# A two-layer image kernel: planes stored once, loads of 16 rows, and the calls of slots 0 to 6 in another order on three engines

## The chip, the core and the metric

The kernel runs on one core of a Trainium2 chip. Its time is the device time of one launch in microseconds (us): the median of three runs. The core has TensorE (PE), VectorE (DVE), ScalarE (ACT), GpSimd (POOL) and SyncE (SP), whose queue issues nearly all DMAs here. Each engine works through its own list of instructions in order, and semaphores order them against each other.

## What is computed

Eight images of 128 channels and 64x64 pixels go through two layers. The first splits an image into four bands of 32x32 (Haar), runs a sparse attention with 8 heads on the low band, a depthwise and a 1x1 convolution with group norms on the other three, puts the bands together and adds a feed-forward part. The second is a full attention over all 4096 pixels with queries and keys of 16 numbers.

```
# layer 0, the attention on the low band: N = 1024, 8 heads, hd = 16
q = _l2norm(q); k = _l2norm(k)
attn = einsum('bhnd,bhmd->bhnm', q, k) * hd ** -0.5
_, idx = top_k(attn, N // 2)          # keep 512 of 1024 per row
attn = where(mask(idx), attn, -1e9)
out = einsum('bhnm,bhmd->bhnd', softmax(attn), v)
...
# layer 1: n = 4096, R = 16
q = einsum('rc,bcn->bnr', Wq, xf) + bq
k = einsum('rc,bcn->brn', Wk, xf) + bk[:, None]
v = einsum('oc,bcn->bon', Wv, xf) + bv[:, None]
attn = softmax(einsum('bnr,brm->bnm', q, k) / 4.0)
out = einsum('bcm,bnm->bcn', v, attn)
out = gamma[0] * (einsum('oc,bcn->bon', Wo, out) + bo[:, None]) + xf
```

## The kernel before

**Stages.** The work of layer 0 for image b runs together with that of layer 1 for image b−1. The program is: `between(0,0)` (opens image 0), `slots(0)` (layer 0 alone), a loop over six images of `between(b-1,b)` and `slots(b)`, the same two once more for the last image, then `between` (closes layer 0 of the last image) and `slots(8)` (layer 1 alone). `between` does all that is not attention: the convolutions, the norms, the feed-forward part, and the projections of queries, keys and values of both layers. `slots` has eight slots and what follows them. Slot h takes head h of layer 0 and chunk h of layer 1: 512 of the 4096 queries.

**Precision.** Queries and keys are split into three bf16 planes whose sum is the fp32 value. A score is the sum of six products of planes, named by `TERMS` as pairs (plane of q, plane of k), so a matmul contracts over 6x16 = 96 rows, written to DRAM from the planes and read back in the order of `TERMS` (QK0 for layer 0, `work` in the trace's names; QP1 and KP1, `QP` and `KP`, for layer 1). Three more rows hold the threshold of a query in layer 0 (from TPT) and its maximum in layer 1 (from MPT), so that the exponential's argument comes out of the matmul itself: 99 rows.

**A head of layer 0**, the calls and the line each has in the trace. PE `score(h,i)` (L446), i = 0 to 7, makes 128x1024 scores; ACT `evict(h,i)` (L1175) copies them out with their sum. DVE `centre(h,k)` (L1671, T<-SUM) makes a first threshold of half k, that is of tiles 4k to 4k+3, from those sums; ACT `count(h,round,i)` (L1183) counts the scores above it in three rounds, and DVE `update` (L1701) moves it. DVE `apart` (L1743), `excess` (L1726, L1729), `flip` (L1751) and `eight` (L1760) find the eight scores nearest to it; `match`, `middle` and `threshold` (to L1843) the exact one. PE `turn` (L490), ACT `turned` (L1217) and three DMAs (L368) bring it as TPT's rows into QK0. Then PE `half_t` (L514) makes the scores again, now turned, ACT `half_e` (L1235) takes the exponential, DVE `half_m` (L1857) sets it to zero below the threshold, and PE `weigh` (L524) multiplies by the values.

**A chunk of layer 1.** PE `maxima(h,k)` (L548), k = 0 to 31, makes 128x512 scores and DVE `maxima` (L1928) reduces them to a maximum. Both go through one PSUM bank, so PE's next one waits for DVE's reduction. DVE `parts`, PE `maxrow` (L555), ACT `maxrow` (L1251, writes MPT) and three DMAs (L324) bring the maxima into QP1. Then PE `l1_score(h,j)` (L566), j = 0 to 15, ACT `l1_exp` (L1243) and PE `l1_weigh(h,j)` in two halves of eight matmuls (L582); in the end DVE `l1_norm` (L1950), PE `l1_turn` (L594) and DVE `l1_out` (L1960), and SP stores the output (L337).

**What sets the order.** Nobody schedules: each engine's list is written out by hand as calls. For slots 0 to 6 of images 1 to 7 that is `search` and the loop body that follows it on PE, a loop body on ACT, and `search` on DVE; they hold calls of four neighbouring heads and chunks. `first`, `closing`, `alone` and `chunks` are other lists, for the rest. `score` waits for a free pair of two PSUM banks that it shares with `half_t`, and `l1_score` has two other pairs. SP's list in a slot is: TPT's rows, loads of layer 1's input, MPT's rows for the next chunk, `load_head(h+3)` (L279), the store of finished output. In `between` SP stores layer 0's planes (`store_planes`, L286), loads heads 0 to 2, stores layer 1's planes (L406), loads QP1 and KP1 (L410), and stores X1 (L413).

## Time and profile before

| | |
|---|---|
| median of three runs | 5667.28 us |
| lowest and highest | 5665.16 and 5668.21 us |
| span of the profiled execution | 5667.7 us |
| one image (`between` and eight slots) | 668 us |
| one of the 49 slots, `l1_out` to `l1_out` | 63.7 to 63.8 us, up to 64.7 |
| granted TensorE clock, mean; in the slot read | 0.91; 1.00 |
| DMA over the span | 35 GB/s of mean traffic, 200 MB |

The profile is one execution; its span is the time from the first to the last instruction and stands 0.4 us over the median of the runs. Busy times are sums per engine; DMA-issuing and waiting instructions do not count as busy. A slot is read best along DVE, from one `l1_out` to the next.

### The profile page before, as it was taken

What the parts mean: (1) busy time and instruction counts of PE and PEld (TensorE: products, weight loads), DVE (VectorE), ACT (ScalarE), POOL (GpSimd) and SP (SyncE); (2) the same over time, 40 slices, a digit from 0 to 9 for tenths busy, and PEclk for the clock granted to TensorE, in tenths of its full rate; (3) what the DMA queues carried; (4) which work ended last, traced back from release to release, by engine and by line L of the source; (5) the groups of instructions that cost most, each with busy time, mean ns of one, the idle gap of its engine ahead of it and who ended that gap; (6) DMA issues with size and microseconds to landing.
All of it is one profiled execution on the core that took longest, in us unless ns stands there. A gap on an engine that the chain in (4) does not pass through costs nothing.

```text
span 5667.7 us, 92692 instructions
## 1 busy us (share of the span) xinstructions
PE 4766.2 (84%) x30180; PEld 3123.3 (55%) x30180; DVE 4618.9 (81%) x9087; ACT 4256.4 (75%) x6779; POOL 250.6 (4%) x125
## 2 busy tenths in 40 slices
PE   4444899988999889988999889998899889997799
PEld 2001366654666456663666546664466636664588
DVE  4887799987999789986999879997799879996553
ACT  3883699948998499966999489884899669994333
POOL 2001000010000200010000100002000100000000
PEclk7555799998999989998999989999899989998899
DMA  1001200012001110012000120011100120001100
GB/s 68 7 11 50 74 15 16 15 56 76 16 20 43 59 43 18 16 61 74 15 15 13 58 76 16 20 43 50 51 16 18 59 75 15 15 13 43 36 12 16
DMA packets 104805, 199.97 MB, mean 35 GB/s; under 512 B 36632, under 2 KB 41656, under 8 KB 100184
## 3 DMA queue, kind: packets, MB, share of 16 engines
q1 hardware_dynamic: 104280, 193.56, 11.1%
q8 instruction: 257, 4.21, 0.3%
q14 instruction: 268, 2.20, 0.1%
HBM read 110.61 MB, written 82.05 MB: 34 GB/s over the span
## 4 chain that ended last, share of the span: by engine, by line
PE 41%; DVE 23%; ACT 15%; issue 14%; SPq 3%; DMA 3%; DVEq 0%; ACTq 0%; POOL 0%; POOLq 0%
PE PS L582 16%; ACT work L1183 7%; PE PS L548 5%; DVE M L1760 4%; DVE MX L1928 4%; PE PS L566 4%; ACT work L1243 3%; DVE work L1751 3%; PE PS L514 3%; PE PS L524 3%; DVE work L1743 2%; PE PS L1057 2%; ACT arena L1175 2%; DVE arena L1857 2%; DMA work<-TPT 1%
## 5 line engine op out<-in xcount | busy, mean ns | idle before, releaser
L582 PEld LDWEIGHTS PS<-V,work 128*128 128x128 f32 x16384 | 2106.7, 193 | 155.8 <-issue 7.0
L582 PE MATMUL PS<-V,work 128*128 128x129 f32 x16384 | 2125.2, 277 | 2.5 <-ACT work L1243 1.2
L1183 ACT ACTIVATE work<-arena,T 128x1024 bf16<-128x1024 f32 x1504 | 1725.8, 1150 | 22.7 <-DVE T L1671 18.8
L1928 DVE TENSOR_REDUCE MX<-PS 128x1 f32<-128x512 f32 x2048 | 1399.3, 687 | 249.6 <-PE PS L548 233.9
L1243 ACT ACTIVATE work<-PS 128x1024 f32<-128x1024 f32 x1024 | 1046.8, 1024 | 334.0 <-PE PS L566 332.3
L548 PE MATMUL PS<-KP,QP 96*128 96x512 bf16 x2048 | 845.5, 414 | 137.3 <-DVE MX L1928 95.3
L566 PE MATMUL PS<-QP,KP 99*128 99x512 bf16 x2048 | 624.6, 387 | 77.5 <-ACT work L1243 54.2
L1175 ACT ACTIVATE arena<-PS 128x1024 f32<-128x1024 f32 x512 | 523.2, 1022 | 216.7 <-PE PS L446 209.5
L1857 DVE SCALAR_TENSOR_TENSOR arena<-PS,work 128x512 f32<-128x512 f32 x896 | 606.2, 684 | 67.3 <-ACT work L1235 65.3
L1760 DVE MAX8 M<-work 128x8 f32<-128x512 f32 x1024 | 648.4, 682 | 1.0
L1235 ACT ACTIVATE work<-PS 128x512 f32<-128x512 f32 x896 | 530.8, 601 | 119.9 <-PE PS L514 116.1
L548 PEld LDWEIGHTS PS<-KP,QP 96*128 96x128 bf16 x2048 | 200.5, 98 | 543.8 <-DVE MX L1928 419.1
L446 PE MATMUL PS<-work 96*128 96x512 bf16 x1024 | 350.5, 428 | 175.2 <-ACT arena L1175 167.2
L514 PE MATMUL PS<-work 99*128 99x512 bf16 x896 | 337.3, 388 | 93.7 <-DVE arena L1857 54.2
L1743 DVE TENSOR_SCALAR work<-arena,T 128x1024 f32<-128x1024 f32 x512 | 378.4, 745 | 2.3
L1751 DVE TENSOR_SCALAR work<-work,FL 128x1024 uint32<-128x1024 uint32 x512 | 375.9, 747 | 1.0
L524 PE MATMUL PS<-arena,VT 128*17 128x256 f32 x4096 | 321.4, 411 | 10.0 <-DVE arena L1849 5.8
L566 PEld LDWEIGHTS PS<-QP,KP 99*128 99x128 bf16 x2048 | 185.0, 99 | 222.6 <-ACT work L1243 126.5
L1183 ACT ACTIVATION_READ_ACCUMULATOR work<-arena,T 128x1 f32 x1504 | 302.9, 201 | 0.0
L446 PEld LDWEIGHTS PS<-work 96*128 96x128 bf16 x1024 | 80.4, 102 | 329.9 <-ACT arena L1175 272.2
L514 PEld LDWEIGHTS PS<-work 99*128 99x128 bf16 x896 | 83.2, 98 | 222.1 <-DVE arena L1857 127.0
L2614 POOL TENSOR_TENSOR work<-work 128x1024 f32<-128x1024 f32 x8 | 22.5, 2814 | 3509.9 <-DMA work<-in_x 3509.9
(193 smaller groups left out, 4160.8 us busy)
## 6 DMA issues: line engine op xcount, KB each, us to landing
scr<-work SPq DMA_DIRECT2D x96, 256.0 KB
work<-scr SPq DMA_DIRECT2D x128, 192.0 KB, 2.8
work<-in_x SPq DMA_DIRECT2D x16, 1024.0 KB, 7.7
arena<-in_x SPq DMA_DIRECT2D x8, 2048.0 KB, 9.9
scrX<-arena SPq DMA_DIRECT2D x8, 2048.0 KB, 14.2
XR<-scrX SPq DMA_DIRECT2D x64, 256.0 KB, 2.8
out<-YO SPq DMA_DIRECT2D x64, 256.0 KB, 2.0
scrL<-work SPq DMA_DIRECT2D x24, 512.0 KB, 2.6
```

Source lines behind the costliest of these rows:

```text
L514: mm(PS[:, c, :], kp(h)[0:KA, 128 * mt:128 * mt + 128], qp(h)[0:KA, 512 * c:512 * c + 512], start=True, stop=True).then_inc(s["st" if c el ...
L548: mm(PS[:, maxbank(c, k, l0), :], QP1[0:KS, c * 512 + 128 * i:c * 512 + 128 * i + 128], KP1[0:KS, 512 * w:512 * w + 512], start=True, stop ...
L566: last = mm(PS[:, pairbanks(k, l0) + t, :], KP1[0:KA, 128 * mt:128 * mt + 128], QP1[0:KA, j * 512:j * 512 + 512], start=True, stop=True)
L582: last = mm(PS[:, 5 + i // 2, 136 * (i % 2):136 * (i % 2) + 129], P1[:, (16 * j + k) % 3, t, 128 * i:128 * i + 128], V1[:, mt, :], start=( ...
L1175: A(scores(h, i), bank2(0), ACT.Copy, scale=0.25, accum_out=SUM[:, h % 2, i:i + 1]).then_inc(s["eva"], 1)
L1183: A(junk[:, m % 2, :], scores(h, i), ACT.Sign, scale=-1.0, bias=T[:, h % 2, i:i + 1], accum_out=CA[:, h % 2, i:i + 1]).then_inc(s["ca"], 1)
L1235: A(JA[:, mt % 2, 512 * c:512 * c + 512], PS[:, c, :], ACT.Exp, scale=0.25).then_inc(s["e" if c else "eh"], 1)
L1243: A(P1[:, (16 * j + k) % 3, :, :].rearrange("p t n -> p (t n)"), PS[:, u:u + 2, :].rearrange("p a n -> p (a n)"), ACT.Exp, scale=0.25).the ...
L1751: cp.did(V.tensor_scalar(JDu[:, c, :], JDu[:, c, :], FL[:, h % 2, i:i + 1].bitcast(u32), None, ALU.bitwise_xor))
L1760: cp.did(V.max(M8[:, i, a, :], JD[:, c, 512 * a:512 * a + 512]))
L1857: V.scalar_tensor_tensor(scores(h, mt)[:, 512 * c:512 * c + 512], PS[:, c, :], 0.0, JA[:, mt % 2, 512 * c:512 * c + 512], ALU.is_ge, ALU.m ...
L1928: V.reduce_max(MX[:, c % 2, i, w:w + 1], PS[:, maxbank(c, k, l0), :], AX.X).then_inc(s["mr"], 1)
```

## The change

**A, layer 0's planes.** `TERMS` has another order. `scr0` holds each plane once, so three stores of 128 rows x 4 KB take the place of twelve, and each head is loaded by 12 DMAs of 16 rows x 2 KB, one for each plane of each term, instead of two of 96 rows. PE's waits for a head count 192 instead of 32. For head 0 the loads of planes 0 and 1 (ten) start when these two have landed, and plane 2's two parts are copied from the planes in SBUF. Heads 1 and 2 are loaded behind layer 1's loads.

**B, layer 1's planes.** `scr1` is [3, 32, 4096]; each plane is stored by four DMAs when it is made, and QP1 and KP1 are loaded by 12 DMAs of 16 rows x 8 KB: the ten parts of planes 0 and 1 when those have landed, then the two of plane 2. Before, 12 DMAs of 16 rows x 4 pieces of 2 KB were issued when all three planes had landed.

**C, the call lists** of the 49 slots on PE, ACT and DVE hold the same calls in another order (116, 66 and 88 calls). The other lists are unchanged.

```diff
-TERMS = [(0, 0), (0, 1), (1, 0), (1, 1), (0, 2), (2, 0)]
+TERMS = [(0, 0), (0, 1), (0, 2), (1, 0), (1, 1), (2, 0)]
-        scr0 = nc.dram_tensor("scr0", [2, NH, len(TERMS), HD, N0], bf16, kind="Internal").ap()
-        scr1 = nc.dram_tensor("scr1", [3, 128, N0], bf16, kind="Internal").ap()
+        scr0 = nc.dram_tensor("scr0", [3, 128, 2, N0], bf16, kind="Internal").ap()
+        scr1 = nc.dram_tensor("scr1", [3, 32, N1], bf16, kind="Internal").ap()
-            def load_head(h):
+            def load_head(h, parts=(0, 1, 2)):
                 done = s["hq%d" % (h % 3)]
-                for w in range(2):
-                    sp.dma_start(QK0[0:KS, h % 3, w, :], scr0[w, h].rearrange("j d n -> (j d) n")).then_inc(done, 16)
+                d = slice(HD * h, HD * h + HD)
+                for j, pair in enumerate(TERMS):
+                    for w, t in enumerate(pair):
+                        if t in parts:
+                            sp.dma_start(QK0[HD * j:HD * j + HD, h % 3, w, :], scr0[t, d, w, :]).then_inc(done, 16)
+            def load_planes(parts):
+                for w, dst in ((1, KP1), (0, QP1)):
+                    for j, pair in enumerate(TERMS):
+                        if pair[w] in parts:
+                            sp.dma_start(dst[HD * j:HD * j + HD], scr1[pair[w], HD * w:HD * w + HD, :]).then_inc(s["qp1"], 16)
+            def store_plane(n, t, made):
                 sp.wait_ge(s[made], (n + 1) * 2)
+                sp.dma_start(scr0[t].rearrange("p w n -> p (w n)"), PT[:, t, :]).then_inc(s["scrw"], 16)
+            def head0_late():
                 for j, pair in enumerate(TERMS):
+                    for w, t in enumerate(pair):
+                        if t == 2:
+                            sp.dma_start(QK0[HD * j:HD * j + HD, 0, w, :], PT[0:HD, 2, w * N0:w * N0 + N0]).then_inc(s["hq0"], 16)
...
                 if opn:
-                    store_planes(n, 0, "p0")
-                    store_planes(n, 1, "p1")
-                    store_planes(n, 2, "p2")
+                    store_plane(n, 0, "p0")
+                    store_plane(n, 1, "p1")
                     sp.wait_ge(s["vt"], (n + 1) * 2)
                     sp.sem_inc(s["free"], 1)
-                    sp.wait_ge(s["scrw"], (n + 1) * 192)
-                    for h in range(3):
+                    sp.wait_ge(s["scrw"], n * 48 + 32)
+                    load_head(0, (0, 1))
+                    store_plane(n, 2, "p2")
+                    head0_late()
+                if fin:
+                    for a, made in enumerate(("p10", "p11", "p12")):
+                        sp.wait_ge(s[made], f + 1)
+                        for j in range(4):
+                            sp.dma_start(scr1[a][:, N0 * j:N0 * j + N0], PT1[32 * j:32 * j + 32, a, :])                                .then_inc(s["scrw1" if a < 2 else "scry1"], 16)
+                    sp.wait_ge(s["scrw1"], (f + 1) * 128)
+                    load_planes((0, 1))
+                    sp.wait_ge(s["scry1"], (f + 1) * 64)
+                    load_planes((2,))
+                if opn:
+                    sp.wait_ge(s["scrw"], (n + 1) * 48)
+                    for h in range(1, 3):
                         load_head(h)
...
@@ PE, tail of a slot
+                    l1_weigh(h - 1, 15, (0,))
+                    last_weigh(h, 7)
+                    l1_weigh(h - 1, 15, (1,))
                     maxrow(h)
-                    last_weigh(h, 7)
-                    l1_weigh(h - 1, 15, (0,))
-                    l1_weigh(h - 1, 15, (1,))
...
                     score(h + 1, 0)
...
                     l1_turn(h - 1)
+                    score(h + 1, 1)
...
```

How the three lists change where one slot ends and the next begins. ACT, from the next to last `half_e` of a head to the first exponential of the next chunk (L1235 `half_e`, L1183 `count`, L1251 `maxrow`, L1175 `evict`, L1243 `l1_exp`), before:

```order
L1235 ACTIVATE work<-PS 128x512
L1182 REGISTER_ALU
L1183 ACTIVATE work,CA<-arena,T 128x1024
L1235 ACTIVATE work<-PS 128x512
L1250 REGISTER_ALU
L1251 ACTIVATE MPT<-PS 12x128
L1203 ISA
L1175 ACTIVATE arena,SUM<-PS 128x1024
L1240 REGISTER_ALU
L1243 ACTIVATE work<-PS 128x1024
```

After, from the last `half_e` (L1247 there; L1194 `count`, L1263 `maxrow`, L1186 `evict`, L1255 `l1_exp`):

```order
L1247 ACTIVATE work<-PS 128x512
L1193 REGISTER_ALU
L1194 ACTIVATE work,CA<-arena,T 128x1024
L1193 REGISTER_ALU
L1194 ACTIVATE work,CA<-arena,T 128x1024
L1193 REGISTER_ALU
L1194 ACTIVATE work,CA<-arena,T 128x1024
L1262 REGISTER_ALU
L1263 ACTIVATE MPT<-PS 12x128
...
L1186 ACTIVATE arena,SUM<-PS 128x1024
L1252 REGISTER_ALU
L1255 ACTIVATE work<-PS 128x1024
```

Three counts now stand between the last `half_e` and MPT's copy. The rows left out are the first of two evictions and what waits ahead of each, so two evictions now stand ahead of the exponential. DVE, from the last part of `l1_norm` (L1950) over `l1_out` (L1960) to `centre` of the next head (L1671), before:

```order
L1950 TENSOR_TENSOR ON<-PS,RD 128x256 x2
L1685 REGISTER_ALU
L1726 TENSOR_SCALAR EC<-CA 128x4
L1729 TENSOR_SCALAR FL<-EC 128x4
L1760 MAX M<-work 128x8 x2
L1960 SCALAR_TENSOR_TENSOR YO<-PS,gbo,XR 128x512
L1743 TENSOR_SCALAR work<-arena,T 128x1024
L1928 TENSOR_REDUCE MX<-PS 128x1
L1751 TENSOR_SCALAR work<-work,FL 128x1024 x2
...
L1928 TENSOR_REDUCE MX<-PS 128x1
L1692 ISA
L1671 TENSOR_SCALAR T<-SUM 128x4
```

After (each line number is 12 higher):

```order
L1962 TENSOR_TENSOR ON<-PS,RD 128x256 x2
L1755 TENSOR_SCALAR work<-arena,T 128x1024
L1697 REGISTER_ALU
L1738 TENSOR_SCALAR EC<-CA 128x4
L1741 TENSOR_SCALAR FL<-EC 128x4
L1755 TENSOR_SCALAR work<-arena,T 128x1024
L1972 SCALAR_TENSOR_TENSOR YO<-PS,gbo,XR 128x512
L1763 TENSOR_SCALAR work<-work,FL 128x1024
L1940 TENSOR_REDUCE MX<-PS 128x1
...
L1940 TENSOR_REDUCE MX<-PS 128x1
L1704 ISA
L1683 TENSOR_SCALAR T<-SUM 128x4
```

Both `apart` calls are ahead of `l1_out`, and `centre` stands behind the second reduction, where it stood behind the fourth. PE, from the last `half_t` of a head (L514) to the second score of the next (L446), before:

```order
L514 MATMUL PS<-work 128x512
L555 MATMUL PS<-identb,MP 12x128
L573 REGISTER_ALU
L582 MATMUL PS<-V,work 128x129 x8
L524 MATMUL PS<-arena,VT 17x256 x12
L473 REGISTER_ALU
L446 MATMUL PS<-work 128x512 x2
L594 MATMUL PS<-cons,ON 128x128 x4
L562 REGISTER_ALU
L566 MATMUL PS<-QP,KP 128x512 x2
...
L463 REGISTER_ALU
L446 MATMUL PS<-work 128x512 x2
```

After (each line number is 17 higher):

```order
L599 MATMUL PS<-V,work 128x129 x8
L572 MATMUL PS<-identb,MP 12x128
L490 REGISTER_ALU
L463 MATMUL PS<-work 128x512 x2
L541 MATMUL PS<-arena,VT 17x256 x12
L611 MATMUL PS<-cons,ON 128x128 x4
L480 REGISTER_ALU
L463 MATMUL PS<-work 128x512 x2
L541 MATMUL PS<-arena,VT 17x256 x4
...
L579 REGISTER_ALU
L583 MATMUL PS<-QP,KP 128x512 x2
```

The halves of `l1_weigh` (L599) are ahead of `maxrow` (L572), the first score (L463) is right behind it, and `l1_score` (L583) comes last.

## Rows read from the trace of the kernel before

**Rows 1.** the page: the span; busy time by engine.

```profile
span 5667.7 us, 92692 instructions
...
PE 4766.2 (84%) x30180; PEld 3123.3 (55%) x30180; DVE 4618.9 (81%) x9087; ACT 4256.4 (75%) x6779; POOL 250.6 (4%) x125
```

**Rows 2.** stretches: length; busy PE, PEld, DVE, ACT, POOL; granted clock, DMA share, GB/s.

```profile
961.68:991.96 30.28, 26.75 (x185) 18.74 (x184) 28.79 (x62) 28.69 (x48) 0.00 (x0) 1.00 0.06 19
991.96:997.56 5.60, 4.77 (x35) 3.74 (x33) 3.78 (x10) 5.35 (x10) 0.00 (x0) 1.00 0.01 2
997.56:1025.51 27.95, 27.25 (x215) 19.32 (x213) 26.52 (x55) 25.21 (x44) 0.00 (x0) 1.00 0.07 19
961.68:1025.51 63.83, 58.77 (x430) 41.79 (x428) 59.09 (x123) 59.25 (x100) 0.00 (x0) 1.00 0.06 17
```

**Rows 3.** DVE's waits, 997.56 to 1025.51: for whom, us, times, longest.

```profile
DVE MX L1928 <- PE PS L548: 1.1, 2, 0.8
DVE YO L1960 <- PE PS L594: 0.3, 1, 0.3
DVE arena L1857 <- ACT work L1235: 0.3, 1, 0.3
```

**Rows 4.** timeline of DVE, same slot: start, us, line, operation.

```profile
961.68 0.75 DVE L1960 SCALAR_TENSOR_TENSOR YO<-PS,gbo,XR 128x512 f32<-128x512 f32 x1
962.35 0.74 DVE L1743 TENSOR_SCALAR work<-arena,T 128x1024 f32<-128x1024 f32 x1
...
970.43 0.16 DVE L1671 TENSOR_SCALAR T<-SUM 128x4 f32<-128x4 f32 x1
```

**Rows 5.** timeline of ACT, same slot; in brackets idle before, releaser.

```profile
957.37 0.61 ACT L1235 ACTIVATE work<-PS 128x512 f32<-128x512 f32 x1
957.84 0.25 ACT L1251 ACTIVATE MPT<-PS 12x128 bf16<-12x128 f32 x1
960.79 1.02 ACT L1175 ACTIVATE arena<-PS 128x1024 f32<-128x1024 f32 x1 [2.70 <-PE PS L446]
...
968.38 0.20 ACT L1175 ACTIVATION_READ_ACCUMULATOR arena<-PS 128x1 f32 x1
...
992.86 1.13 ACT L1183 ACTIVATE work<-arena,T 128x1024 bf16<-128x1024 f32 x1
...
996.59 0.60 ACT L1235 ACTIVATE work<-PS 128x512 f32<-128x512 f32 x1 [0.25 <-PE PS L514]
```

**Rows 6.** timeline of SP's DMA issues, same slot: MPT's rows, load_head.

```profile
958.12 1.97 SPq L324 DMA_DIRECT2D QP<-MPT  x3
960.21 0.83 SPq L279 DMA_DIRECT2D work<-scr  x2
```

**Rows 7.** timelines, image 1's first slot: MPT's copy, l1_score waiting for its rows.

```profile
699.41 0.27 ACT L1251 ACTIVATE MPT<-PS 12x128 bf16<-12x128 f32 x1 [0.98 <-PE PS L555]
...
702.87 1.03 PE L566 MATMUL PS<-QP,KP 99*128 99x512 bf16 x2 [2.61 <-DMA QP<-MPT]
```

**Rows 8.** timeline of PE, same slot: l1_score, and a half of l1_weigh.

```profile
961.48 0.60 PE L566 MATMUL PS<-QP,KP 99*128 99x512 bf16 x2
...
1019.04 1.06 PE L582 MATMUL PS<-V,work 128*128 128x129 f32 x8
```

**Rows 9.** timelines, last boundary: first and last load (SP), PE's wait.

```profile
5273.74 0.33 SPq L410 DMA_DIRECT2D QP<-scr  x1
...
5278.80 0.43 SPq L410 DMA_DIRECT2D KP<-scr  x1
...
5288.58 1.01 PE L548 MATMUL PS<-KP,QP 96*128 96x512 bf16 x2 [13.08 <-DMA KP<-scr]
```

**Rows 10.** timelines at the boundaries of images 0, 2 and 3.

```profile
108.86 1.00 ACT L1175 ACTIVATE arena<-PS 128x1024 f32<-128x1024 f32 x1
...
1338.21 0.59 PE L548 MATMUL PS<-KP,QP 96*128 96x512 bf16 x2 [0.47 <-ACT V L1484]
...
1975.20 1.03 PE L446 MATMUL PS<-work 96*128 96x512 bf16 x2 [2.93 <-DMA work<-scr]
```

More of the change, by code:

```diff
@@ L694, in search @@
                     l1_score(h - 1, 10)
                     half_t(h - 1, 1, 1)
+                    maxima(h, 20)
+                    l1_weigh(h - 1, 9, (1,))
+                    half_t(h - 1, 2, 0)
+                    maxima(h, 21)
                     weigh(h - 1, 0)
-                    maxima(h, 21)
-                    l1_weigh(h - 1, 9, (0,))
-                    half_t(h - 1, 2, 0)
+                    weigh(h - 1, 1)
+                    half_t(h - 1, 2, 1)
                     maxima(h, 22)
-                    l1_weigh(h - 1, 9, (1,))
@@ L702, in search @@
-                    half_t(h - 1, 2, 1)
-                    maxima(h, 23)
-                    weigh(h - 1, 1)
                     l1_score(h - 1, 11)
                     half_t(h - 1, 3, 0)
-                    maxima(h, 24)
+                    maxima(h, 23)
                     l1_weigh(h - 1, 10, (0,))
                     half_t(h - 1, 3, 1)
+                    maxima(h, 24)
+                    l1_weigh(h - 1, 10, (1,))
                     maxima(h, 25)
-                    l1_weigh(h - 1, 10, (1,))
@@ L1387, in slots @@
                     half_e(h - 1, 2, 1)
+                    count(h, 2, 0)
+                    l1_exp(h - 1, 11)
+                    half_e(h - 1, 3, 0)
+                    half_e(h - 1, 3, 1)
                     count(h, 2, 1)
-                    half_e(h - 1, 3, 0)
-                    l1_exp(h - 1, 11)
-                    half_e(h - 1, 3, 1)
                     count(h, 2, 2)
+                    count(h, 2, 3)
                     half_e(h - 1, 4, 0)
@@ L2043, in search @@
                     apart(h, 4)
+                    maxima(h + 1, 1)
+                    centre(h + 1, 0)
+                    apart(h, 5)
                     maxima(h + 1, 2)
-                    apart(h, 5)
+                    flip(h, 5)
                     maxima(h + 1, 3)
-                    centre(h + 1, 0)
-                    flip(h, 5)
+                    eight(h, 5)
                     maxima(h + 1, 4)
-                    eight(h, 5)
+                    flip(h, 4)
                     maxima(h + 1, 5)
-                    flip(h, 4)
+                    eight(h, 4)
```

227 lines of the change are left out of this document (99 added, 128 removed).

## The prediction

> **What bounds the kernel now.** I read the page first, then the busy time by stretch, then the waits of VectorE (DVE), and last the timelines of the engines and of the DMA queue. The page shows three engines busy for most of a span of 5667.7 us, and none of them full [rows 1]. Of the span, 49 pieces of some 63.8 us are the slots that the change reorders: slots 0 to 6 of images 1 to 7, where a head of the first attention runs beside a chunk of the second. I cut one of them at three points of DVE. In all of it DVE, ScalarE (ACT) and TensorE (PE) work 59 us of 63.8 [rows 2], so no engine alone is the bound and the gain must come from idle time that the order causes. The stretches differ. From `l1_out` to the end of `threshold` DVE runs 30.28 us without an idle stretch worth naming. From there to the first `half_m` it takes 5.60 us, during which TPT's rows go by DMA and ACT's `half_e` follows. From there to the next `l1_out` it takes 27.95 us, and DVE waits for 1.1 us on `maxima`, 0.3 on `half_e` and 0.3 on `l1_turn`: 1.7 us in all [rows 3].
>
> **The call lists (part C).** The calls are the same and only their places differ, so I follow the cycle along DVE and price each stretch.
>
> Front stretch. `apart(h,3)` stood behind `l1_out`; now it stands ahead of it. An instruction of its size holds DVE for 0.67 us until the next [rows 4]: −0.66 here, +0.66 in the back stretch. `centre(h+1,0)` moves from behind the fourth `maxima` to behind the second and comes 1.9 us sooner in the list. It needs the sum of `evict(h+1,3)`. In before that accumulator is read at 968.38 and done by 968.6, against a `centre` at 970.43 [rows 4, 5]: a margin of 1.85 us, which the move uses up. Where does the eviction end after the change? In before the copy of MPT is started right behind the last `half_e` (957.37, then 957.84); in after three `count` of 1.13 us stand between [rows 5], so the copy starts 3.4 us behind that `half_e`'s end. The rows then reach QP1 by three DMAs (958.12, 1.97 us for the issues [rows 6]). How long until `l1_score` can start shows where PE waits for nothing else: 699.41 to 702.87, 3.46 us [rows 7]; in the slot above it is 3.64 (961.48 [rows 8]). From the end of that `half_e` this makes 3.4 + 3.46 = 6.9 us to `l1_score(h,0)`. On DVE the way from the same point to `l1_out` is a `half_m`, two `eight`, `l1_norm`, two `apart` and `excess`: at 0.67 us for each large instruction, 1.2 for `l1_norm` and 0.35 for `excess`, 4.9 us. So `l1_score(h,0)` starts 2.0 us behind `l1_out`, where in before it started 0.2 ahead of it. Behind it ACT has 0.5 us until the exponential starts, then exp, evict 2, exp, evict 3: with 0.9 and 1.0 us a piece evict 3 ends about 6.5 us behind `l1_out`. DVE gets to `centre` after `l1_out`, two `flip`, one `apart` and two `maxima` (each 0.6 to 0.7) and two `eight` of 1.2: 6.24 us. The wait is then 0.26 us plus the 0.1 us of the semaphore: +0.36. On the other side the gap of 2.70 us that ACT had ahead of evict 0 (960.79 [rows 5]) goes: the counts fill it. It is not won as such, since two new gaps of about 1.2 us come ahead of evict 1 and of the first exponential.
>
> Middle stretch. `l1_exp(h-1,9)` now stands behind the three counts and right ahead of `half_e(0,0)`. In before that `half_e` starts at 996.59 after a wait of 0.25 [rows 5]. With 0.9 us of exponential in between, less the 0.15 us by which `turned` comes sooner and the 0.35 of slack, it starts 0.4 later. `half_m` has 0.3 us of slack behind it, since DVE was in a reduction: +0.1 to +0.3, taken as +0.2.
>
> Back stretch. PE has two halves of `l1_weigh` fewer ahead of `half_t(7,1)` in the sum of the moves (1.06 us each in the row, 0.9 until the next [rows 8]), and one half of slot work fewer ahead of `l1_turn`. So PE should no longer be what DVE waits for at the end: the 0.3 us of `l1_turn` goes whole. Of the other 1.4 us I take half. Nothing in the lists removes the reason for these waits: one PSUM bank holds `maxima`, so that PE and DVE take turns, and only the distance between two calls hides that. So −1.0, with a bound of −1.7 if all goes and 0 if the waits only change place. What is next if they go is DVE itself.
>
> Sum of a slot: −0.66 + 0.36 + 0.2 + 0.66 − 1.0 = −0.44 us. With 49 slots this is −21.6 us. The bounds are: no `centre` wait and all waits gone, 0.2 − 1.7 = −1.5 (−73.5 us); rows of MPT 1 us later and half the waits gone, +0.56 (+27 us).
>
> **Loads and stores of the first attention (part A).** In a slot the DMA queue of SyncE (SP) issues 12 loads for head h+3 instead of two. At the spacing of 0.47 us that the small loads of a boundary show (12 from 5273.74 to 5278.80 [rows 9]) this is 5.6 us instead of 0.83 [rows 6]. The instruction behind it in SP's list is a store of finished output, whose buffer is not needed for two chunks, and the rows of TPT come 30 us later: 0. The load itself is wanted three slots later, 190 us. The MPT copies are issued ahead of it, but the 12 loads may still be in flight while MPT's packets move; that is in the rival on MPT below. Before a first slot, head 0's rows now land sooner. In the first image this buys nothing: evict 0 starts at 108.86 without any idle time of ACT ahead of it [rows 10]. At the boundary that opens image 3 `score(0,0)` waits 2.93 us for the load [rows 10], and what stands behind it on PE holds up ACT's copies of V; I count 2 of the 2.93: −2 us once. The other images hide it. Heads 1 and 2 now come behind the second attention's loads, 24 issues or 11 us in all, and the store of X1 behind them too. The first score of head 1 and the first use of the stored X1 stand late in the list of the image's first slot, which hides them while it lasts longer than these 11 us and the landing: 0.
>
> **Loads of the second attention (part B).** At the last boundary nothing covers them: PE waits 13.08 us until 5288.58 [rows 9]. From the first issue that is 14.84 us for 12 loads of 128 KB, 1.24 us each, 106 GB/s. In after the stores of the first two planes are out before the third is made, and the first load is issued about 2.9 us behind the third plane, against 3.44. If the pace stays, the term is −0.5; if it becomes the pace of the issues, 0.47, the last lands near 8 us behind the first issue and the term is −6.8. I take −0.5, because bytes and rows of a load are the same as in the rows. The Trainium skill, page "SBUF — State Buffer", section "Door 1: The DMA port swizzle", says that what a transfer reaches is set by how many of 16 ports its partitions lie on, and gives 104 GB/s for 16 partitions; the 106 of this trace agrees. [...] At the other boundaries the first `maxima` waits 0.47 us for ACT's V (1338.21 [rows 10]) and not for the loads: 0.
>
> Sum: 5667.7 − 21.6 − 0.5 − 2 = **5643.6 us**; the profiled execution is 0.4 us over the median of the three runs, so it needs no correction. I say 5644.
>
> **Rivals.**
> *The idle time goes whole.* For it: DVE and ACT stand at 59 of 63.8 us, so there is room, and ACT's largest gap is filled. Against it: the two new gaps on ACT, and the single bank. −1.5 a slot: 5667.7 − 73.5 − 2.5 = 5592 us. Chance 0.13.
> *The idle time only moves.* For it: each slot is a ring through all three engines; what DVE loses less to `maxima` it loses at `centre` and in the middle stretch, where 0.56 us is already counted. Then a slot stays at 63.8 and only the boundaries give: 5665 us. Chance 0.19. That the change does not do what it says falls here too, since the calls are the same.
> *Slower: MPT's rows come late.* Place: the copy of MPT behind three counts, its DMAs, `l1_score(h,0)`, then the exponential and evictions 2 and 3, and `centre`, which has no margin any more. Every part of a us that this chain takes longer than 3.4 + 3.46 stands whole in DVE's list, 49 times. For it: 3.64 is shown in the slots, the loads of 16 rows run near it, and PE's own moves (`score(h+1,1)` and `weigh` 6 ahead of `l1_score`) hold it back further. Against it: DVE's other waits would shrink in exchange. It decides from 0.44 us more than I count; with 1.0 us it gives +0.56 × 49 − 2.5 = +25: 5693 us. Chance 0.20.
>
> **How the numbers follow.** Forecast 0.48, with its own range of 5620 to 5662 (per slot −0.1 to −0.9). Faster by over 0.2% (11 us, about what a measurement of this kernel can tell from no change) means under 5656: 0.13 and 0.43 of the forecast's 0.48, 0.56. Within 0.2%: 0.19 and 0.05, 0.24. Slower: 0.20. The range is to leave out 2 in 10: from 5602, which leaves out most of the first rival, to 5693, which leaves out half of the last.
>
> **What would show it.** Right: `l1_out` to `l1_out` in 63.2 to 63.5 us; ACT's gap ahead of evict 0 gone, and gaps of 1 us ahead of evict 1 and the first exponential; PE waiting 0.7 to 1 us for MPT's rows in 49 slots; DVE waiting 0.2 to 0.5 us at `centre` for ACT; its waits on `maxima` in the back stretch halved; PE's last wait for KP1 at 12.6 us. Wrong: a wait at `centre` of over 0.8 us (the slower rival), or no wait there and slots of 62.3 (the first); a wait of PE for KP1 at the last boundary of 6 to 7 us (loads that overlap); new waits for head 1's rows or for scrX at the start of an image.

## The result and the profile after

The changed kernel took 5648.18 us in the median of ten runs (5641.8 to 5656.94), the kernel before 5664.41 us (5655.12 to 5670.76) in its ten. The ratio is 0.9971 with an interval of 0.9963 to 0.9979: 16 us faster. 5644 was forecast, 24 us below the 5668 it started from, with a range of 5602 to 5693. The profiled execution's span is 5655.1 us, against 5667.7 [rows 1], so the two traces show 12.6 us of the difference.

The page of the changed kernel, its span and busy times:

```profile
span 5655.1 us, 93339 instructions
...
PE 4812.5 (85%) x30180; PEld 3107.4 (55%) x30180; DVE 4598.7 (81%) x9087; ACT 4258.7 (75%) x6779; POOL 250.5 (4%) x125
```

The same slot as in [rows 2], cut at the same three points of DVE: `l1_out`, the end of `threshold`, the first `half_m`, the next `l1_out`. The columns are as there.

```profile
957.29:987.00 29.71, 28.32 (x195) 19.76 (x193) 28.22 (x61) 28.31 (x45) 0.00 (x0) 1.00 0.08 24
987.00:992.40 5.40, 4.16 (x27) 3.00 (x28) 3.78 (x9) 5.08 (x10) 0.00 (x0) 1.00 0.02 2
992.40:1020.18 27.78, 27.11 (x211) 18.52 (x209) 26.54 (x55) 25.61 (x44) 0.00 (x0) 1.00 0.05 14
957.29:1020.18 62.89, 59.59 (x430) 41.28 (x428) 58.54 (x122) 59.01 (x98) 0.00 (x0) 1.00 0.06 17
```

The slot lasts 62.89 us instead of 63.83, and each of its three stretches is shorter. Read over the whole trace by the 64 starts of `l1_out`, the difference of 12.6 us is made of a gain and two losses, summed over seven images. (The periods are named by the `l1_out` they run from and to. The first six `l1_out` of an image stand in the new lists, 0.66 us later than before by the move of `apart(h,3)`, the last two in the closing lists.)

| stretch | before, us | after, us | difference |
|---|---|---|---|
| first to seventh `l1_out`, 42 periods | 2691.4 | 2644.8 | −46.6 |
| of it: they start 0.66 us later and end where they did | | | −4.6 |
| seventh to eighth (the closing lists begin) | 412.1 | 429.8 | +17.7 |
| eighth to the next image's first (the boundary) | 1528.9 | 1545.0 | +16.1 |
| of it: six of them end 0.66 us later | | | +4.0 |
| before the first (it ends 0.66 us later too) | 768.7 | 768.9 | +0.2 |

So these slots gave 42 us, 1.0 us each, and 30 us of it were given back at the ends of the images and at the boundaries. Slot 0 of an image lies inside a boundary (or, once, before the first `l1_out`) and is not among the 42. From the end of its threshold to its `l1_out` it took 33.5 us before and 33.2 after, so the boundaries' loss lies ahead of that point. Means of the 42 periods: the front stretch went from 30.24 to 29.63 us, the middle one from 5.76 to 5.43, the back one from 28.08 to 27.92.

DVE at that slot's start and at `centre` (L1683; before, [rows 4]); PE's first `l1_score` (before, [rows 8]); ACT from the last `half_e` (L1247) over MPT's copy (L1263) to the accumulator of evict 3 (before, [rows 5]):

```profile
957.29 0.75 DVE L1972 SCALAR_TENSOR_TENSOR YO<-PS,gbo,XR 128x512 f32<-128x512 f32 x1 [0.30 <-PE PS L611]
...
963.51 0.17 DVE L1683 TENSOR_SCALAR T<-SUM 128x4 f32<-128x4 f32 x1
```

```profile
958.60 0.60 PE L583 MATMUL PS<-QP,KP 99*128 99x512 bf16 x2
```

```profile
951.41 0.60 ACT L1247 ACTIVATE work<-PS 128x512 f32<-128x512 f32 x1 [0.45 <-PE PS L531]
...
955.30 0.25 ACT L1263 ACTIVATE MPT<-PS 12x128 bf16<-12x128 f32 x1
955.46 1.00 ACT L1186 ACTIVATE arena<-PS 128x1024 f32<-128x1024 f32 x1
...
957.72 1.02 ACT L1186 ACTIVATE arena<-PS 128x1024 f32<-128x1024 f32 x1 [1.17 <-PE PS L463]
...
959.24 1.02 ACT L1255 ACTIVATE work<-PS 128x1024 f32<-128x1024 f32 x1 [0.41 <-PE PS L583]
...
963.23 0.19 ACT L1186 ACTIVATION_READ_ACCUMULATOR arena<-PS 128x1 f32 x1
```

MPT's copy starts 3.3 us behind the end of the last `half_e` (3.4 were forecast), and the 2.70 us gap ahead of evict 0 is gone, as forecast. Of the two new gaps, forecast at about 1.2 us each, the one ahead of evict 1 is 1.17 us and the one ahead of the exponential 0.41. The accumulator is ready at 963.42 and `centre` starts at 963.51, without a wait: the two meet to within 0.1 us. In the second period of the first six images (the second slot, below) the rows of MPT take longer, and `centre` waits 0.2 to 0.5 us. PE (first row) and DVE (second) in that of image 2, between 1494.97 and 1558.46:

```profile
1496.89 0.60 PE L583 MATMUL PS<-QP,KP 99*128 99x512 bf16 x2 [0.65 <-DMA QP<-MPT]
...
1501.74 0.17 DVE L1683 TENSOR_SCALAR T<-SUM 128x4 f32<-128x4 f32 x1 [0.47 <-ACT arena L1186]
```

This period is 63.49 us where its neighbours are 62.59 and 62.60. At the end of an image the lists of the slots meet the closing lists, which are the same as before. `l1_score` of the last chunk there (image 3):

```profile
2475.36 0.61 PE L583 MATMUL PS<-QP,KP 99*128 99x512 bf16 x2 [1.29 <-DMA QP<-MPT]
```

Before, `l1_score` started there 0.4 us ahead of the seventh `l1_out` (2480.28 against 2480.65); now 1.6 us behind it (2475.36 against 2473.72), and behind it come only exponentials and weighings of this chunk. The seventh to eighth `l1_out` lasts 59.57 us here, 58.11 before.

### The profile page after: what moved, and what is told of

Read it like the earlier page. It is cut to its first block, busy times and chain, and to the rows that moved or that the text cites. A ratio compares the mean times of both kernels' runs of the same rounds, so it can differ in the third digit from the quotient of the medians.

```text
span 5655.1 us, 93339 instructions
## 1 busy us (share of the span) xinstructions
PE 4812.5 (85%) x30180; PEld 3107.4 (55%) x30180; DVE 4598.7 (81%) x9087; ACT 4258.7 (75%) x6779; POOL 250.5 (4%) x125
## 4 chain that ended last, share of the span: by engine, by line
PE 39%; DVE 32%; issue 14%; ACT 11%; SPq 2%; DMA 2%; DVEq 1%; POOL 0%; ACTq 0%; POOLq 0%
PE PS L599 15%; DVE MX L1940 8%; DVE M L1772 5%; PE PS L565 5%; PE PS L583 4%; ACT work L1194 3%; DVE work L1755 3%; DVE work L1763 3%; PE PS L531 2%; PE PS L541 2%; DVE arena L1869 2%; ACT work L1255 2%; PE PS L1068 2%; PE PS L463 2%; ACT arena L1186 1%
## 5 line engine op out<-in xcount | busy, mean ns | idle before, releaser
L599 PEld LDWEIGHTS PS<-V,work 128*128 128x128 f32 x16384 | 2113.7, 193 | 156.5 <-ACT work L1255 24.1
L599 PE MATMUL PS<-V,work 128*128 128x129 f32 x16384 | 2138.1, 277 | 2.5 <-ACT work L1255 1.2
L1194 ACT ACTIVATE work<-arena,T 128x1024 bf16<-128x1024 f32 x1504 | 1711.4, 1141 | 17.6 <-DVE T L1683 11.6
L1255 ACT ACTIVATE work<-PS 128x1024 f32<-128x1024 f32 x1024 | 1040.0, 1017 | 337.9 <-PE PS L583 326.6
L565 PE MATMUL PS<-KP,QP 96*128 96x512 bf16 x2048 | 845.2, 414 | 159.2 <-DVE MX L1940 118.1
L583 PE MATMUL PS<-QP,KP 99*128 99x512 bf16 x2048 | 624.0, 386 | 68.5 <-ACT work L1255 47.0
L1247 ACT ACTIVATE work<-PS 128x512 f32<-128x512 f32 x896 | 510.3, 592 | 182.8 <-PE PS L531 176.1
L1186 ACT ACTIVATE arena<-PS 128x1024 f32<-128x1024 f32 x512 | 523.9, 1023 | 116.3 <-PE PS L463 106.3
L565 PEld LDWEIGHTS PS<-KP,QP 96*128 96x128 bf16 x2048 | 200.3, 98 | 555.9 <-DVE MX L1940 476.9
L463 PE MATMUL PS<-work 96*128 96x512 bf16 x1024 | 352.9, 430 | 127.8 <-ACT arena L1186 126.0
L583 PEld LDWEIGHTS PS<-QP,KP 99*128 99x128 bf16 x2048 | 174.2, 99 | 247.3 <-ACT work L1255 158.0
L1194 ACT ACTIVATION_READ_ACCUMULATOR work<-arena,T 128x1 f32 x1504 | 291.3, 194 | 0.0
L463 PEld LDWEIGHTS PS<-work 96*128 96x128 bf16 x1024 | 75.9, 102 | 268.2 <-ACT arena L1186 226.7
L541 PEld LDWEIGHTS PS<-arena,VT 128*17 128x17 f32 x4096 | 89.2, 99 | 185.7 <-issue 136.3
```

The lines of the kernel that those rows point to most:

```text
L565: mm(PS[:, maxbank(c, k, l0), :], QP1[0:KS, c * 512 + 128 * i:c * 512 + 128 * i + 128], KP1[0:KS, 512 * w:512 * w + 512], start=True, stop ...
L583: last = mm(PS[:, pairbanks(k, l0) + t, :], KP1[0:KA, 128 * mt:128 * mt + 128], QP1[0:KA, j * 512:j * 512 + 512], start=True, stop=True)
L599: last = mm(PS[:, 5 + i // 2, 136 * (i % 2):136 * (i % 2) + 129], P1[:, (16 * j + k) % 3, t, 128 * i:128 * i + 128], V1[:, mt, :], start=( ...
L1186: A(scores(h, i), bank2(0), ACT.Copy, scale=0.25, accum_out=SUM[:, h % 2, i:i + 1]).then_inc(s["eva"], 1)
L1194: A(junk[:, m % 2, :], scores(h, i), ACT.Sign, scale=-1.0, bias=T[:, h % 2, i:i + 1], accum_out=CA[:, h % 2, i:i + 1]).then_inc(s["ca"], 1)
L1255: A(P1[:, (16 * j + k) % 3, :, :].rearrange("p t n -> p (t n)"), PS[:, u:u + 2, :].rearrange("p a n -> p (a n)"), ACT.Exp, scale=0.25).the ...
```

## The experiments

Each kernel is compared with the kernel before on the same chip; "six" is the sum of the 42 periods, "end" that of the seven from the seventh to the eighth `l1_out`, "boundary" that of the seven behind it, all from the kernel's one trace.

| kernel | ratio (interval) | span | six | end | boundary |
|---|---|---|---|---|---|
| before | 1 | 5667.7 | 2691.4 | 412.1 | 1528.9 |
| changed | 0.9971 (0.9963 to 0.9979) | 5655.1 | 2644.8 | 429.8 | 1545.0 |
| lists alone | 0.9965 (0.9951 to 0.9979) | 5652.3 | 2648.2 | 430.0 | 1537.0 |
| planes and loads alone | 0.9996 (0.9986 to 1.0006) | 5669.2 | 2694.8 | 407.7 | 1529.0 |
| copy early | 0.9928 (0.9908 to 0.9947) | 5634.3 | 2649.1 | 411.4 | 1536.3 |
| exponential 9 back | one run, 5640.8 us | 5639.0 | 2643.7 | 424.3 | 1536.6 |
| copy early at the end only | 0.9944 (0.9929 to 0.9959) | 5639.4 | 2647.4 | 423.8 | 1528.7 |
| two `l1_weigh` back | 1.0072 (1.0053 to 1.0092) | 5703.0 | 2700.1 | 429.4 | 1538.7 |
| copy later | 1.0064 (1.0045 to 1.0083) | 5698.7 | 2679.9 | 426.5 | 1556.3 |
| copy early, exponential back | 0.9945 (0.9929 to 0.9960) | 5633.8 | 2644.0 | 416.1 | 1537.6 |
| DVE's two moves back | 1.0309 (1.0286 to 1.0331) | 5821.1 | 2792.4 | 425.7 | 1563.9 |
| `l1_weigh(14)` back | one run, 5689.0 us | 5687.2 | 2681.4 | 431.8 | 1539.1 |
| `l1_weigh(8)` back | one run, 5672.2 us | 5670.4 | 2666.8 | 429.9 | 1538.1 |
| lists alone, copy early | 0.9928 (0.9911 to 0.9945) | 5621.6 | 2643.2 | 414.9 | 1528.7 |

**Lists alone.** The kernel before with the new call lists.

> The kernel before with the new call lists of the three engines alone; planes, stores and loads as before. In the changed kernel's trace the 42 periods from the first to the seventh l1_out of an image lasted 46.5 us less in sum, and the stretch from the seventh to the eighth, whose lists are unchanged, 1.5 us more per image where TensorE's clock was alike. Theory 1 (the lists make the whole gain, the loads are hidden): ratio 0.9965 to 0.998 to the kernel before, slots of 62.3 to 63.0 us, and the 1.5 us at the image's end are here too. Theory 2 (the 12 small loads per head cost something, since MPT's rows go through the same DMA engines): this kernel is faster than the changed one, 0.993 to 0.996, the periods of 63.2 to 63.5 that the changed kernel has in second slots are 62.6 here, and PE waits for MPT's rows less.

The ratio is that of the changed kernel, the slots and the ends are too (2648.2 and 430.0 us). Theory 1 holds as far as the intervals tell: the lists make the gain, and the loss at the ends.

**Planes and loads alone.** The kernel before with parts A and B of the change.

> The kernel before with planes stored once and the new loads alone; the call lists as before. Theory 1: 0.9995 (the boundary's -2.5 us), so no difference that can be told, slots of 63.7 to 63.8. PE's last wait for the loads of KP1 and QP1 11.4 us as in the changed kernel, against 13.1. Theory 2 (the small loads disturb the rows of MPT and TPT): slots of 64 us and more, ratio 1.001 to 1.004.

No difference that can be told, in the total or in the slots. PE's last wait for KP1 and QP1 is 11.1 us here, where 11.4 was expected. At the last boundary the loads go more slowly than they are issued. SP and PE there in the changed kernel, as in [rows 9]:

```profile
5261.31 3.52 SPq L288 DMA_DIRECT2D KP<-scr  x5
...
5267.64 0.42 SPq L288 DMA_DIRECT2D QP<-scr  x1
...
5275.22 1.01 PE L565 MATMUL PS<-KP,QP 96*128 96x512 bf16 x2 [11.44 <-DMA QP<-scr]
```

The wait fell from 13.08 to 11.44 us. From the first issue to PE's start it is 13.9 us instead of 14.84, 113 GB/s, so the 12 loads still go at 1.16 us each, although neighbours now lie on other rows of the tile. They did not take the pace of the issues, by which the term was to be −6.8 us. The rate stayed near the 104 GB/s that the Trainium skill (page "SBUF — State Buffer", section "Door 1: The DMA port swizzle") gives for a transfer of 1 MiB to 16 partitions.

**Copy early.** The changed kernel, ACT's copy one count sooner, in every slot and ahead of the closing list:

```diff
                 for h in range(-1, NH):
-                    maxrow(h - 1)
                     evict(h, 0)
...
                     count(h, 2, 6)
+                    maxrow(h)
                     count(h, 2, 7)
                 closing()
```

(and the call at the start of ACT's `closing()` goes).

> The changed kernel with ScalarE's copy of MPT moved ahead of the last of the three counts that stand before it, 1.13 us earlier, in every slot and ahead of the closing list too. Theory 1 (the late copy is what the change pays for: PE waits 1.29 us for MPT's rows ahead of the closing list, and 0.65 us in second slots): the seventh to eighth l1_out takes 1.1 us less than in the changed kernel, second slots 0.5 us less, the other slots stay at 62.3 to 62.9; sum -7.5 - 3 = -10 us against the changed kernel, ratio about 0.9953 to the kernel before. Theory 2 (slots are a ring in which waits only move): within 3 us of the changed kernel.

It is 18 us faster than the changed kernel, with an interval clear of it. PE's first `l1_score` ahead of the closing list waits 0.47 us instead of 1.29:

```profile
2465.32 0.61 PE L583 MATMUL PS<-QP,KP 99*128 99x512 bf16 x2 [0.47 <-DMA QP<-MPT]
```

The end period is 58.2 to 58.8 us in five images of seven, 57.8 in the last and 61.2 in one; the usual one of the changed kernel is 59.6 to 59.8, so 1.2 us went, as expected. The slots' sum gained nothing (2649.1 against 2644.8). Of the seven second slots four shrank by 0.1 to 0.5 us, and three took 64.3 to 64.4, longer than in the changed kernel: the clock fell in these three. Two windows of 4 us, 32 us behind the start of a second slot of 64.33 us and of one of 63.02:

```profile
865.58:869.58 4.00, 3.22 (x12) 2.52 (x13) 1.45 (x3) 2.98 (x6) 0.00 (x0) 0.60 0.03 2
1524.38:1528.38 4.00, 3.21 (x23) 2.29 (x23) 2.82 (x6) 4.00 (x8) 0.00 (x0) 1.00 0.03 2
```

The granted clock is the third figure from the end: 0.60 of full speed in the first, which is the lower level (1.2 of 2.4 GHz) for most of the window, with 12 matmuls done instead of 23. The same window of the other two long slots shows 0.61 and 0.60, and over the whole slot the mean granted clock is 0.97 in these three and 1.00 in the other four. PE's work in the 4 us ahead is the same in both slots shown (busy for 3.27 and 3.28 us, at full clock). So second slots with an even clock are 0.1 to 0.5 us shorter, and the expected 0.5 us is reached in one of them only. Part of what differs between these traces is where the clock falls, which the section on the hardware takes up.

**Exponential 9 back.** `l1_exp(h-1,9)` ahead of `turned(h-1)` again on ACT.

> The changed kernel with l1_exp(h-1,9) back ahead of turned(h-1) on ScalarE. The prediction had its move cost 0.2 us a slot, because half_e(0,0) comes later by it: by that this kernel's middle stretch (threshold's end to the first half_m) is 5.2 us and the slots 0.2 us shorter. The reading of the changed kernel's trace: the middle stretch is 5.40 us because the reductions of maxima set it, and half_e has room: by that it stays at 5.4 (TPT's rows come 0.3 us later and still land before half_t needs them), or grows to 5.6 if they don't.

In the one trace the middle stretch is 5.51 us in the mean (5.43 in the changed kernel) and the six periods 1.1 us shorter in sum. The move that the prediction priced at 0.2 us a slot is worth nothing that can be told.

**Copy early at the end only.** As copy early, but with `if h == NH - 1:` ahead of the new call, and the old place in the other slots.

> The changed kernel with the copy of MPT moved ahead of the last count only where the closing list follows, once per image; in the other slots it stays behind the three counts. The kernel with the copy early in all slots gained 18 us on the changed one, all of it between the seventh and eighth l1_out (429.8 to 411.4 us over seven images) and nothing in the slots (2644.8 to 2649.1 for the six). Theory 1 (the image's end alone pays for the late copy): the same 411 us here, slots as in the changed kernel, ratio 0.992 to 0.9945 to the kernel before. Theory 2 (the gain came from elsewhere, such as where TensorE's clock drops): the seventh to eighth l1_out keeps values of 62 to 65 us in some images, ratio 0.995 to 0.998.

The ratio lies where theory 1 put it, but the trace speaks for a mixture. The end is 58.4 and 58.6 us in two images, 57.9 in the last, and 61.3 to 62.6 in four. What is shown: one move per image wins about 12 us (5635.7 against 5648.2 us, each beside its own runs of before). What part of that is the 1.2 us an image by which the undisturbed ends are shorter (8 us), and what part the clock's places, the runs don't separate.

**Two `l1_weigh` back.** The PE moves that the prediction's back stretch rests on, undone.

```diff
-                    l1_weigh(h - 1, 8, (1,))
                     half_t(h - 1, 0, 0)
                     maxima(h, 18)
+                    l1_weigh(h - 1, 8, (1,))
...
                     l1_weigh(h - 1, 14, (0,))
-                    half_t(h - 1, 7, 1)
                     l1_weigh(h - 1, 14, (1,))
+                    half_t(h - 1, 7, 1)
```

> The changed kernel with two moves of the PE list undone: l1_weigh(14,(1,)) back ahead of half_t(7,1), and l1_weigh(8,(1,)) back behind maxima(18). The prediction had these moves free PE ahead of DVE's waits (-0.7 of the -1.0 us in the back stretch). By it the back stretch grows by 0.5 to 0.9 us (the half of 0.9 us stands in PE's way again) and the middle one from 5.4 to 5.6 us or more, since half_t waits for TPT's rows with maxima behind it: +0.7 to +1.1 us a slot, ratio 1.001 to 1.006 times 0.997. Rival: the gain of the slots comes from DVE's and ACT's moves, PE has room, and the slots stay within 0.1 us.

It is 58 us slower than the changed kernel and slower than before. The same slot as above:

```profile
959.80:989.94 30.14, 28.28 (x195) 19.75 (x193) 28.33 (x61) 28.31 (x45) 0.00 (x0) 1.00 0.09 23
989.94:995.33 5.39, 3.76 (x23) 2.60 (x24) 3.86 (x9) 5.04 (x9) 0.00 (x0) 1.00 0.02 2
995.33:1023.87 28.54, 27.55 (x214) 19.05 (x212) 26.75 (x55) 25.80 (x44) 0.00 (x0) 1.00 0.05 13
```

The means of the 42 periods are 29.98, 5.41 and 28.91. The back stretch grew by 0.99 us and the front one by 0.35, for `centre` now waits (6.56 us from `l1_out` against 6.28). The middle did not grow. These two moves cost more than the whole change gained, so undoing them does not tell what share of the gain was theirs: the lists depend on each other.

**Copy later.** ACT's copy of MPT behind `evict(h,0)`, the slower rival made on purpose.

> The changed kernel with ScalarE's copy of MPT one step later still, behind evict(h,0), 0.9 us. It is the slower rival of the prediction, made on purpose. By it the lateness stands whole in every slot, since l1_score(h,0) waits for the rows, the exponentials and evictions 2 and 3 follow, and centre waits for them: 0.6 to 0.9 us in each of 42 slots and 0.9 at each image's end, sum +30 to +45 us, ratio 1.002 to 1.005 to the kernel before; the first centre 6.8 to 7.3 us behind l1_out instead of 6.28. If ScalarE's exponentials have room in the slots, only the second slots and the image ends grow: +10 us, ratio about 0.999.

53 us slower than the changed kernel; the slots take 0.84 us more each (2679.9 against 2644.8), for 0.9 us that the copy was moved. That is the rival's price, and the changed kernel stands right at the point from which it decides. Of the rest, 11 us lie at the boundaries in the traces. The way is not only the one the rival named, since the copy also frees the PSUM bank. PE in one slot of it:

```profile
2297.18 1.13 PE L611 MATMUL PS<-cons,ON 128*128 128x128 f32 x8 [0.53 <-ACT MPT L1263]
...
2300.09 0.60 PE L583 MATMUL PS<-QP,KP 99*128 99x512 bf16 x2 [0.47 <-DMA QP<-MPT]
```

`l1_turn` (L611) waits for the copy and `l1_out` for `l1_turn` (0.9 us in this slot); of the 0.84 us, 0.47 lie in the back stretch (27.92 to 28.39) by that way, and 0.33 in the front one by MPT's rows.

**Copy early, exponential back.** Both edits.

> Both edits together: the copy of MPT ahead of the last count in all slots, and l1_exp(h-1,9) back ahead of turned(h-1), in the changed kernel. The second took 1 us off the slots' sum in its one profile (2644.8 to 2643.7 us) and nothing else that has a mechanism. Expected: as with the early copy alone, 0.9928 with its interval of 0.991 to 0.995; a theory in which the exponential's place matters would give 0.2 us a slot, 8 us or 0.0015 more.

The ratio lies between those of the changed kernel and of copy early, and its interval overlaps that of copy early. The slots are 5 us shorter in the trace (2644.0 against 2649.1), but no second slot of this trace met a fall of the clock, and three of copy early did. There is no sign that the exponential's place matters.

**DVE's two moves back.**

```diff
-                    apart(h, 3)
                     l1_out(h - 1)
+                    apart(h, 3)
...
                     maxima(h + 1, 1)
-                    centre(h + 1, 0)
                     apart(h, 5)
                     maxima(h + 1, 2)
                     flip(h, 5)
                     maxima(h + 1, 3)
+                    centre(h + 1, 0)
```

> The changed kernel with two moves of the DVE list undone: apart(h,3) behind l1_out again, and centre(h+1,0) behind the fourth maxima. By the prediction the first is worth nothing (0.66 us from one stretch to the other) and the second takes away a wait of 0.36 us a slot: 15 us faster than the changed kernel, ratio 0.9945. By the changed kernel's trace DVE does not wait at centre except in second slots (6.28 us from l1_out to the first centre on average, where 6.22 is its work alone): 0 to -3 us from that; and if the later centre, 1.9 us, holds up ScalarE's counts, up to +1 us a slot.

A large miss of both readings: 3.1% slower, 190 us against the changed kernel. The front stretch is 33.05 us in the mean instead of 29.63. In the slot from 2203.96 to 2270.82, ACT behind its third exponential, and then DVE's `centre`:

```profile
2213.63 1.15 ACT L1194 ACTIVATE work<-arena,T 128x1024 bf16<-128x1024 f32 x1 [2.23 <-DVE T L1683]
```

```profile
2213.36 0.16 DVE L1683 TENSOR_SCALAR T<-SUM 128x4 f32<-128x4 f32 x1
```

ACT's first `count` stands ahead of evict 4 in the new list and waits 2.23 us for `centre`; evict 4 and all counts behind it come later by that. PE and DVE behind it:

```profile
2215.93 0.60 PE L463 MATMUL PS<-work 96*128 96x512 bf16 x2 [2.40 <-ACT arena L1186]
```

```profile
2216.79 0.69 DVE L1940 TENSOR_REDUCE MX<-PS 128x1 f32<-128x512 f32 x1 [2.08 <-PE PS L565]
```

PE's `score` (L463) waits for the eviction, `maxima` (L565) stands behind it in PE's list, and DVE waits 2.08 us for that. The new order of ACT needs the early `centre`. Which part of the 3.4 us the place of `apart` makes was not tried by itself.

**`l1_weigh(14)` back** and **`l1_weigh(8)` back**, each of the two PE moves alone.

> The changed kernel with one PE move undone: l1_weigh(14,(1,)) back ahead of half_t(7,1). Both PE moves undone gave slots 1.3 us longer, 1.0 of it in the back stretch and 0.35 in the front one. Expected if this move is the one: back stretch 28.8 to 28.9 us, front 29.9, middle 5.4, six periods 2695 to 2700 us in sum over seven images. Rival: the two are needed together, half of it each.

> The changed kernel with the other PE move undone: l1_weigh(8,(1,)) back behind maxima(18), which puts half_t(0,0) 0.9 us earlier in PE's list. In the changed kernel PE does not wait for TPT's rows at half_t(0,0), in the kernel before it waited 0.7 us. Expected: PE waits 0.2 to 0.5 us there again, with maxima(18) behind it, and the middle stretch grows from 5.43 to 5.6 or 5.8 us. The kernel with both undone had a middle stretch of 5.41 us, which speaks against this: then it stays.

The first makes 0.87 us a slot (six 2681.4): front 29.97, middle 5.52, back 28.35. It costs nearly as much in the front stretch, at `centre` (6.56 us), as in the back one, where all of it was expected. The second makes 0.52 us (2666.8), all in the back stretch (28.49). PE's wait for TPT's rows came back, with the 0.3 us expected, but the middle stretch did not grow (5.40). One by one the two cost 1.39 us, near the 1.32 of both together. PE and DVE in a slot of the second kernel, from its first `half_t`:

```profile
992.35 0.39 PE L531 MATMUL PS<-work 99*128 99x512 bf16 x1 [0.31 <-DMA work<-TPT]
...
993.06 1.06 PE L599 MATMUL PS<-V,work 128*128 128x129 f32 x8
993.95 0.38 PE L531 MATMUL PS<-work 99*128 99x512 bf16 x1
```

```profile
995.00 0.69 DVE L1869 SCALAR_TENSOR_TENSOR arena<-PS,work 128x512 f32<-128x512 f32 x1 [0.29 <-ACT work L1247]
...
996.62 0.69 DVE L1869 SCALAR_TENSOR_TENSOR arena<-PS,work 128x512 f32<-128x512 f32 x1 [0.33 <-ACT work L1247]
```

The half of `l1_weigh(8)` (993.06) now stands between the first two `half_t`, which start 1.6 us apart, and `half_m` waits for two of the exponentials that follow, 0.6 us in all.

**Lists alone, copy early.** The kernel before with the new lists and the early copy.

> The kernel before with the new call lists and the copy of MPT ahead of the last count, without the new planes, stores and loads. The planes and loads alone gave 0.9996 (interval 0.9986 to 1.0006). If they are worth nothing here too: 0.993 as with them (0.9928, 0.9908 to 0.9947). If the small loads of heads cost something beside the rows of MPT once the slots are tight, it is faster by 1 to 5 us; if their 2 us at the last boundary count, slower by 2.

0.9928, 5625.2 us in the median: 41 us faster than before and, as far as the intervals tell, the same as copy early with the new planes (5629.8). The planes and loads are worth nothing that can be told here either.

## Why the prediction came out right, point by point

The time lies 4 us from the forecast, but that is luck: the sum got there by two errors that cancel. 42 slots gave 42 us, where all 49 were to give 21.6, and the ends of the images and the boundaries took 30 where 2.5 were to be gained. The slot itself came out nearer to the first rival: −1.0 us, outside the forecast's own −0.1 to −0.9, and five of an image's six periods of 62.3 to 63.5 us (62.3 to 62.9 without the second) where 63.2 to 63.5 were to show.

- **`apart(h,3)`, −0.66 and +0.66.** As forecast; in the table above it moves 4.6 us out of the 42 periods, into the boundaries and the stretch before the first `l1_out`.
- **Wait at `centre`, +0.36.** Mis-sized: 6.28 us from `l1_out` in the mean, where DVE's work alone takes 6.22, so +0.06. `l1_score` started 1.3 us behind `l1_out` (958.60) and not 2.0. MPT's rows took 3.30 us from the copy, not 3.46, and the way from the last `half_e` to `l1_out` took 5.3 us, not 4.9, since `l1_turn` is waited for (0.30 us). Only second slots show the mechanism, with 0.2 to 0.5 us.
- **Middle stretch, +0.2.** The sign was wrong: −0.33. The step that failed priced `half_e` alone and put DVE's waits for `maxima` in this stretch at nothing: 1.7 us before. PE and DVE in the kernel before:

```profile
996.09 0.61 PE L514 MATMUL PS<-work 99*128 99x512 bf16 x2 [0.70 <-DMA work<-TPT]
```

```profile
996.95 0.69 DVE L1928 TENSOR_REDUCE MX<-PS 128x1 f32<-128x512 f32 x1 [0.83 <-PE PS L548]
```

`half_t` waited 0.70 us for TPT's rows, `maxima` stood behind it in PE's list, and DVE waited 0.83 us for that, right ahead of `half_m`; `half_e` had been done for some 0.4 us [rows 5]. PE, DVE and ACT in the changed kernel:

```profile
991.15 0.38 PE L531 MATMUL PS<-work 99*128 99x512 bf16 x1
...
991.79 0.69 DVE L1940 TENSOR_REDUCE MX<-PS 128x1 f32<-128x512 f32 x1 [0.57 <-PE PS L565]
992.40 1.28 DVE L1869 SCALAR_TENSOR_TENSOR arena<-PS,work 128x512 f32<-128x512 f32 x2
```

```profile
991.79 1.05 ACT L1247 ACTIVATE work<-PS 128x512 f32<-128x512 f32 x2
```

`half_t` does not wait any more. Over the whole trace PE's waits for TPT's rows at these `half_t` fell from 39.4 us in 49 waits to 1.0 in one, and DVE's waits for `maxima` in the stretch from 1.99 to 1.65 us in the mean, which is the −0.33. `half_e` has lost its room, since it now ends just as `half_m` starts, but moving the exponential back gives it 0.15 us and gains nothing (exponential 9 back). Which moves did away with the wait for TPT's rows is open in part: with `l1_weigh(8)` back 0.32 of its 0.80 us a slot returned.
- **Back stretch, −1.0.** −0.82, net of `apart`. That PE's moves bear on it is shown: the two halves of `l1_weigh`, put back, cost 1.3 us a slot, 1.0 of it here. What share of the gain they made is not. The waits that were to go stayed for the most part, in the slot read:

```profile
DVE MX L1940 <- PE PS L565: 0.8, 2, 0.6
DVE arena L1869 <- ACT work L1247: 0.2, 1, 0.2
```

```profile
1020.18 0.75 DVE L1972 SCALAR_TENSOR_TENSOR YO<-PS,gbo,XR 128x512 f32<-128x512 f32 x1 [0.47 <-PE PS L611]
```

With `l1_turn`'s 0.47 these are 1.5 us, where there were 1.7 [rows 3]: the waits on `maxima` were not halved, and that for `l1_turn` grew. The rest of the gain is in no listed wait. DVE's busy time of the slot fell too, from 59.09 to 58.54 us for the same calls, and why was not read out.
- **The slower rival.** Its mechanism is real and its price right (0.84 us a slot for 0.9 us). Its place was wrong: the slots stand just at the edge, and the chain decides where the prediction did not look, in the closing lists. The prediction gave each of 49 slots one price and the transition from the changed to the unchanged lists none: it is +1.5 us an image with the clock alike, 10 us in all. The forecast of a wait of 0.7 to 1 us for MPT's rows in 49 slots was wrong too: it is 0.3 to 0.7 us in second slots of six images, under 0.1 in the other slots, and 1.2 to 1.3 at the ends.
- **Parts A and B, −2.5.** Not told from zero, 0.9996. The wait at the last boundary shrank by 1.6 us, between the two bounds and near the one taken. The −2 for head 0 was misread. PE waited for its load in four other boundaries too, 0.75 to 1.3 us each, and in the changed kernel and with planes and loads alone all these waits are gone; yet the boundaries of planes and loads alone sum to 1529.0 us against 1528.9. Something else sets them. Image 3's boundary lasted 224.93 us against 220.77, with a mean granted clock of 0.84 against 0.86.
- **Open:** of the 30 us that came back, 10 are MPT's rows at the ends. The other 7 at the ends and 12 at the boundaries (16.1 less the shift of 4.0) vary from kernel to kernel with the same lists there (1528.7 to 1545.0 us for the boundaries of the changed kernel, of lists alone and of those with the early copy) and go with the clock (mean granted over the six boundaries 0.84 to 0.85 in the changed kernel, 0.85 to 0.88 before); the runs don't show whether the clock makes the length or a longer wait the clock, nor what in the lists, if anything, moves it.

## What to carry to other kernels

When the lists of a steady state are reordered, price the first and last round on their own: they meet lists that were balanced against the old order, and the slack that the steady state hides in may not exist there. Where a round of three engines has little idle time left, look at each hand-over for its margin and not for its wait: some moves of one or two calls cost 0.5 to 3.5 us a round here, and others nothing, when the whole change gained 1.0. Undoing a move in such lists tells that the rest depends on it, not what it gained. An experiment that moves one call by one place, at the transition and in the loop apart, found a version that gains twice as much as the change.
